# A two-block transformer layer on one core: the pieces beside the attention stream and VectorE's order laid out anew

## The reference

```python
# attention, 16 heads of 8
q = q / jnp.maximum(jnp.linalg.norm(q, axis=-1, keepdims=True), EPS_NORM)   # k too
attn = jnp.einsum('bhqd,bhkd->bhqk', q, k) * scale
attn = jax.nn.softmax(attn, axis=-1)
out = jnp.einsum('bhqk,bhkd->bhqd', attn, v)
...
# feed-forward, 352 wide, every operand in blockwise FP4 (blocks of 16 along the last dim)
gate = fp4_linear(x, w_gate)
y = fp4_linear(x, w_up)
h = jax.nn.silu(gate) * y
return fp4_linear(h, w_down)
...
x = x + _L0_attn_ref(xn, ...) + _L0_ffn_ref(xn, ...)
```

## Time and profile before

| | |
|---|---|
| median of 3 runs | 912.56 us (910.73 to 913.38) |
| the profiled execution | 920.16 us, span 918.0 us, mean granted TensorE clock 0.964 |
| attention stream, first to last exponential | 53.6 to 332.2 us |
| busy in that stretch | ScalarE 240.3, TensorE 237.9, VectorE 148.7 us |
| experts | about 430 to 918 us |

### The profile page before, as it was taken

The page is one execution under the profiler, slowest core; times in us unless marked ns, Lnnn a source line. Parts: engine busy times, 40 slices in busy tenths (PEclk is TensorE's granted clock), DMA queues, the critical chain, the costliest instruction groups (busy, mean ns, idle before and its releaser), DMA issues.

```text
span 918.0 us, 15733 instructions
## 1 busy us (share of the span) xinstructions
PE 826.0 (90%) x4516; PEld 519.7 (57%) x4516; DVE 691.6 (75%) x1413; ACT 701.8 (76%) x1165; POOL 35.2 (4%) x41
## 2 busy tenths in 40 slices
PE   4678998998887789897999999999999999999997
PEld 2421222222221139674777777777777777777775
DVE  5885464334556536974999999999999989999997
ACT  3689898998878645554778888787878778878786
POOL 1700000000000000400000000000000000000000
PEclk9969999999999879998999999999999999999999
DMA  4000000000000000007777777787877778778773
GB/s 117 1 1 1 1 2 1 1 1 1 1 1 0 1 1 2 12 30 185 195 190 196 199 194 197 188 198 193 194 199 193 198 183 204 192 198 199 186 203 96
DMA packets 66776, 99.88 MB, mean 109 GB/s; under 512 B 29270, under 2 KB 45942, under 8 KB 66742
## 3 DMA queue, kind: packets, MB, share of 16 engines
q1 hardware_dynamic: 66742, 99.44, 43.0%
HBM read 97.04 MB, written 2.36 MB: 108 GB/s over the span
## 4 chain that ended last, share of the span: by engine, by line
PE 52%; DVE 17%; DMA 12%; ACT 6%; issue 6%; SPq 5%; DVEq 2%; ACTq 0%
DMA wg_raw<-in_L_ffn_w_gate_dram 11%; PE PS L1134 9%; PE PS L1440 5%; PE PS L1442 5%; PE PS L1441 5%; PE PS L1447 5%; PE PS L1449 5%; PE PS L1448 5%; SPq L224 4%; ACT E L446 4%; PE PS L1120 3%; PE PS L1183 3%; DVE HM L1023 2%; ACT SI L581 2%; PE PS L1419 2%
## 5 line engine op out<-in xcount | busy, mean ns | idle before, releaser
L446 ACT ACTIVATE E<-PS 128x1536 f32<-128x1536 f32 x171 | 235.0, 1472 | 35.3 <-PE PS L1120 35.0
L581 ACT ACTIVATE SI<-PS 128x512 f32<-128x512 f32 x320 | 191.5, 599 | 86.6 <-PE PS L1442 86.5
L1023 DVE TENSOR_TENSOR HM<-SI,CWB 128x512 f32<-128x512 f32 x320 | 221.4, 692 | 40.6 <-ACT SI L581 18.1
L1028 DVE TENSOR_TENSOR HLo<-HM,HH 128x512 fp32r<-128x512 f32 x320 | 218.8, 684 | 0.2
L387 ACT ACTIVATE HH<-HM 128x512 fp32r<-128x512 f32 x320 | 199.4, 623 | 3.9 <-DVE HM L1023 3.9
L1134 PE MATMUL PS<-E,VS 128*32 128x512 f32 x1024 | 145.7, 652 | 14.6 <-DVE OS L761 12.7
L1440 PE MATMUL PS<-XH,wgH 128*128 128x512 f32 x320 | 134.4, 420 | 0.0
L1447 PE MATMUL PS<-HH,wdH 128*128 128x512 f32 x320 | 128.2, 400 | 1.2 <-DVE HLo L1028 1.2
L1441 PE MATMUL PS<-XL,wgH 128*128 128x512 f32 x320 | 126.9, 396 | 0.0
L1449 PE MATMUL PS<-HH,wdL 128*128 128x512 f32 x320 | 126.8, 396 | 0.0
L1442 PE MATMUL PS<-XH,wgL 128*128 128x512 f32 x320 | 126.7, 396 | 0.0
(11 more groups left out here) (221 smaller groups left out, 864.9 us busy)
## 6 DMA issues: line engine op xcount, KB each, us to landing
CWB<-combine_weights SPq DMA_DIRECT2D x320, 256.0 KB, 3.9
wg_raw<-in_L_ffn_w_gate_dram SPq DMA_DIRECT2D x80, 64.0 KB, 3.5
wd_raw<-in_L_ffn_w_down_dram SPq DMA_DIRECT2D x80, 64.0 KB, 3.8
X<-in_L_attn_x_dram SPq DMA_DIRECT2D x4, 256.0 KB, 3.6
combine_weights<-CWT SPq DMA_DIRECT2D x2, 512.0 KB, 2.9
out_dram<-X SPq DMA_DIRECT2D x4, 256.0 KB, 2.9
combine_weights<-CWT SPq DMA_DIRECT2D x2, 128.0 KB, 3.8
qkvw_raw<-in_L_attn_qkv_w_dram SPq DMA_DIRECT2D x1, 192.0 KB, 4.2
```

The lines of the kernel that those rows point to most:

```text
L446: nc.scalar.activation(E[:, g % RING, 0:w, :], PS[:, 3 * (g % 2):3 * (g % 2) + w, :], ACT.Exp, scale=SCALE0).then_inc(S["exp_act"], 1)
L581: nc.scalar.activation(SI[:, slot % 2, :], bank(4 + slot % 2), ACT.Silu).then_inc(S["s_act"], 1)
L1023: TT(HM[:, slot % 4, :], SI[:, slot % 2, :], CWB[:, q, half, CH * c:CH * c + CH], ALU.mult)\
L1028: TT(HLo[:, slot % 4, :], HM[:, slot % 4, :], HH[:, slot % 4, :].bitcast(F32), ALU.subtract)\
```

## The change

Three things. First, the places of the pieces: `SHADE_AT` now holds all 62 of them but the last, at most one in a trio, the outputs' too (`OUT_AT` goes); they run from trio 18 to 170. Second, VectorE's calls are in a new order, which follows that of the pieces. Third, `quantise_hidden` is called for one tile at a time, sixteen times, each set between other calls, and `quantise_gate_up` takes the gate's or the up's weights, one at a time. No arithmetic differs, no data move differs, and the second block is not touched. The new `SHADE_AT` keeps the rule that the keys of a head group are replaced only behind the first batch's last scores with them.

```diff
--- before.py
+++ after.py
@@ -256,21 +256,16 @@
 
 
 
-        SHADE_AT = {25: ("k", 0), 28: ("q", 0), 35: ("w", 0), 36: ("w", 1), 39: ("w", 2), 45: ("k", 1), 46: ("q", 1),
-                    49: ("x", 0), 50: ("x", 1), 56: ("g", 0), 57: ("g", 1), 60: ("u", 0), 62: ("u", 1),
-                    66: ("k", 2), 67: ("q", 2), 68: ("g", 2), 70: ("g", 3), 72: ("u", 2), 74: ("u", 3),
-                    77: ("g", 4), 78: ("g", 5), 81: ("u", 4), 82: ("u", 5), 83: ("x", 2), 84: ("x", 3),
-                    88: ("k", 3), 89: ("q", 3), 90: ("g", 6), 92: ("g", 7), 94: ("u", 6), 95: ("u", 7),
-                    98: ("g", 8), 99: ("g", 9), 103: ("u", 8), 104: ("u", 9),
-                    109: ("g", 10), 110: ("g", 11), 113: ("u", 10), 115: ("u", 11),
-                    119: ("g", 12), 121: ("g", 13), 124: ("u", 12), 126: ("u", 13),
-                    130: ("g", 14), 131: ("g", 15), 135: ("u", 14), 136: ("u", 15)}
-        OUT_AT = {after(NB * m + NB + 2): m for m in range(B * GRP - 1)}
-        SHADE = []
-        for g in range(TRIOS):
-            SHADE += [("o", OUT_AT[g])] if g in OUT_AT else []
-            SHADE += [SHADE_AT[g]] if g in SHADE_AT else []
-        SHADE.append(("o", B * GRP - 1))
+        SHADE_AT = {18: ("x", 0), 22: ("w", 2), 24: ("k", 0), 28: ("w", 0), 30: ("o", 0), 34: ("x", 1), 35: ("g", 0),
+                    39: ("q", 0), 42: ("o", 1), 43: ("k", 1), 44: ("w", 1), 46: ("o", 2), 48: ("g", 1), 50: ("u", 0),
+                    54: ("u", 1), 56: ("g", 2), 59: ("u", 2), 62: ("o", 3), 64: ("q", 1), 66: ("g", 3), 67: ("k", 2),
+                    70: ("g", 4), 71: ("o", 4), 72: ("o", 5), 73: ("u", 3), 75: ("u", 4), 77: ("g", 5), 78: ("o", 6),
+                    79: ("x", 2), 80: ("u", 5), 81: ("g", 6), 84: ("q", 2), 86: ("g", 7), 88: ("u", 6), 89: ("g", 8),
+                    91: ("u", 7), 92: ("q", 3), 95: ("g", 9), 97: ("o", 7), 99: ("u", 8), 102: ("g", 10), 103: ("x", 3),
+                    104: ("k", 3), 106: ("o", 8), 107: ("u", 9), 109: ("g", 11), 112: ("u", 10), 114: ("o", 9), 118: ("u", 11),
+                    120: ("g", 12), 122: ("u", 12), 126: ("o", 10), 130: ("g", 13), 141: ("g", 14), 142: ("u", 13), 146: ("o", 11),
+                    150: ("u", 14), 152: ("g", 15), 158: ("o", 12), 162: ("o", 13), 166: ("u", 15), 170: ("o", 14)}
+        SHADE = [SHADE_AT[g] for g in sorted(SHADE_AT)] + [("o", B * GRP - 1)]
         TANH_AT = {g + 1: w[1] for g, w in SHADE_AT.items() if w[0] == "g"}
 
 
@@ -793,9 +788,9 @@
                 quantise(dn, dn, P, I0 // BLK).then_inc(S["fw_dve"], 1)
                 dve.drain()
 
-            def quantise_gate_up():
-                gu = gu_raw[:, :, :].rearrange("p a (b k) -> p (a b) k", k=BLK)
-                quantise(gu, gu, FP, 2 * FA * D // BLK).then_inc(S["fw_dve"], 1)
+            def quantise_gate_up(w):
+                gu = gu_raw[:, FA * w:FA * w + FA, :].rearrange("p a (b k) -> p (a b) k", k=BLK)
+                quantise(gu, gu, FP, FA * D // BLK).then_inc(S["fw_dve"], 1)
                 dve.drain()
 
             def quantise_x(g):
@@ -833,76 +828,109 @@
                     head_T(t)
             square_sums(3)
 
-            def two_tiles(t, m):
-                output(m - 1)
-                gate_out(t)
-                gate_out(t + 1)
-                divide(m - 1)
-                hidden(t)
-                hidden(t + 1)
-
             second_heads(2)
             second_heads(3)
             quantise_down()
             output(0)
-            quantise_gate_up()
-            divide(0)
+            quantise_x(0)
+            inputs_T(0)
+            quantise_gate_up(0)
+            down_weights()
             output(1)
             second_keys(0)
+            quantise_x(1)
+            gate_up_weights(0)
+            quantise_gate_up(1)
+            divide(0)
+            output(2)
+            inputs_T(1)
+            gate_out(0)
+            quantise_x(2)
+            second_queries(0)
             divide(1)
-            second_queries(0)
-            quantise_x(0)
-            output(2)
-            gate_up_weights(0)
+            second_keys(1)
+            output(3)
             gate_up_weights(1)
             divide(2)
-            down_weights()
-            quantise_x(1)
-            output(3)
-            second_keys(1)
+            gate_out(1)
+            hidden(0)
+            quantise_x(3)
+            hidden(1)
+            output(4)
+            gate_out(2)
+            hidden(2)
+            divide(3)
             second_queries(1)
-            divide(3)
-            inputs_T(0)
-            inputs_T(1)
-            quantise_x(2)
-            two_tiles(0, 5)
-            quantise_x(3)
             output(5)
+            gate_out(3)
             second_keys(2)
+            gate_out(4)
+            divide(4)
+            divide(5)
+            hidden(3)
+            hidden(4)
+            output(6)
+            gate_out(5)
+            divide(6)
+            inputs_T(2)
+            hidden(5)
+            gate_out(6)
+            quantise_hidden(0, 1)
             second_queries(2)
-            gate_out(2)
-            divide(5)
-            gate_out(3)
-            hidden(2)
-            hidden(3)
-            two_tiles(4, 7)
-            inputs_T(2)
+            gate_out(7)
+            output(7)
+            hidden(6)
+            gate_out(8)
+            hidden(7)
+            second_queries(3)
+            quantise_hidden(1, 1)
+            gate_out(9)
+            divide(7)
+            output(8)
+            hidden(8)
+            quantise_hidden(2, 1)
+            gate_out(10)
             inputs_T(3)
-            output(7)
             second_keys(3)
-            second_queries(3)
-            gate_out(6)
-            divide(7)
-            gate_out(7)
-            hidden(6)
-            hidden(7)
-            two_tiles(8, 9)
-            quantise_hidden(0, 2)
-            two_tiles(10, 10)
-            quantise_hidden(2, 2)
-            two_tiles(12, 11)
-            quantise_hidden(4, 2)
-            two_tiles(14, 12)
-            quantise_hidden(6, 2)
+            divide(8)
+            hidden(9)
+            output(9)
+            gate_out(11)
+            quantise_hidden(3, 1)
+            hidden(10)
+            divide(9)
+            quantise_hidden(4, 1)
+            hidden(11)
+            output(10)
+            gate_out(12)
+            hidden(12)
+            quantise_hidden(5, 1)
+            divide(10)
+            quantise_hidden(6, 1)
+            output(11)
+            gate_out(13)
+            quantise_hidden(7, 1)
+            quantise_hidden(8, 1)
+            quantise_hidden(9, 1)
             output(12)
+            gate_out(14)
+            quantise_hidden(10, 1)
+            hidden(13)
+            divide(11)
+            quantise_hidden(11, 1)
+            hidden(14)
+            output(13)
+            gate_out(15)
+            residual()
+            quantise_hidden(12, 1)
             divide(12)
-            quantise_hidden(8, 4)
-            output(13)
+            quantise_hidden(13, 1)
+            output(14)
             divide(13)
-            quantise_hidden(12, 4)
-            output(14)
+            quantise_hidden(14, 1)
+            hidden(15)
+            quantise_hidden(15, 1)
             divide(14)
-            residual()
             output(15)
             divide(15)
 
@@ -1160,7 +1188,7 @@
 
             def gate_up_T(w):
                 o = bank_free("w", w)
-                pe.wait_ge(S["fw_dve"], 2)
+                pe.wait_ge(S["fw_dve"], 2 + w * 1)
                 for a in range(FA):
                     last = TR(o[:, FP * a:FP * a + FP], gu_raw[:, FA * w + a, :], ident[0:FP, 0:FP])
                 last.then_inc(S["shade_pe"], 1)
@@ -1184,10 +1212,10 @@
                    start=True, stop=True).then_inc(S["shade_pe"], 1)
 
             def beside(g):
-                if g in OUT_AT:
-                    out_T(OUT_AT[g])
                 kind, n = SHADE_AT.get(g, (None, None))
-                if kind in ("k", "q"):
+                if kind == "o":
+                    out_T(n)
+                elif kind in ("k", "q"):
                     second_heads_T(kind, n)
                 elif kind == "w" and n < 2:
                     gate_up_T(n)
```

## The result

The changed kernel takes 885.67 us (median of 4 runs, 884.38 to 886.92), the kernel before 912.97 (4 runs, 910.73 to 924.28): a ratio of 0.968, 95% interval 0.960 to 0.976. (A ratio compares the executions of both kernels, without the two on record that were marked slow, and not the two medians, whose quotient is 0.970.) A second set of six executions, with a median of 883.88 us beside 17 of the kernel before with 917.57, gave 0.965 (0.961 to 0.970). The forecast was 887, range 879 to 900.

The account below looks back on a forecast made before the run. ScalarE's exponentials were taken to set the attention stream's pace. Its idle falls from 38.0 to 14.1 us (debt, start, VectorE, clock), saving 23.9, plus 1.6 from overlap: 25.5 off the 912.56 median gives 887 us, range 879 to 900.

Parts of the forecast that it names:

- signs named for being right: Attention stream: stage some 253 us, ScalarE's score waits near 14, copy waits under 3, VectorE busy about 174, one-tile block 4.7.
- signs of being wrong: TensorE waiting at bank 7 or for copies at trios 142, 153, 164; half tanh waits; clock under 0.9 behind 240 us.
- debt at TensorE: Attention stream: TensorE work beyond the trio's pace, above 0.85 us of slack, stops ScalarE 7.2 us after, 13.8 before.
- VectorE's lateness: Attention stream after the change: late VectorE work idles ScalarE 0.7 (trio 36), 0.4 (trio 57) and 1.1 us (trios 142, 164).
- clock: Attention stream: falls to the low clock, two on double steps, one or two elsewhere; 4 us charged, bounds 0 and 9.
- TensorE's ledger: Debt added over 171 trios: above 0.85 us, 11.9 us in 26 trios before, 6.2 in 13 after; this part gives 6.6.
- factor of 1.16: Scaling of the ledger's debt, since trios 57 to 112 gave 5.95 us where the trace has 6.9.
- rival of a clock that falls in the quiet tail: Sparse tail of the attention stream: clock falls cost 5 us more than charged, 892 us; chance 0.13.
- The end stays: End of the attention stage: last exponential, two steps, output, transposes and division stay as before.
- VectorE as the bound of the tail: Behind trio 131: VectorE 55 us against ScalarE's 53.6; three late outputs give back 10.5, 897.5 us; chance 0.15.
- no change: Stage behind attention can't use an earlier end: 912 us; chance 0.03.
- the slower case: Bank 7's single order makes outputs 4 to 14 all late at 3.5 us each: 927 us; chance 0.05.

Follow-up runs that it names:

- experiment 9: Changed kernel again: 883.88 us, 0.965; with the residual moved to trio 62: 885.42, 0.968; with tile 0 also quantised at trio 70: 883.17, 0.964.
- experiment 1: Kernel before, with the quantising of the 16 hidden tiles left out: 896.87 us, 0.977 of the kernel before.
- experiment 4: Kernel before, old places of pieces, hidden tiles quantised one by one from trio 104 on, two in a row behind most groups of pieces: 922.64 us, 1.005.
- experiment 10: Kernel before, with the transposes of output 14 moved from trio 165 to the last trio, 170: 918.96 us, 1.004.
- experiment 3: Changed kernel, with hidden tiles quantised in the groups of before (twos and fours), each where its last tile's call stood: 905.07 us, 0.986 of the kernel before.
- experiment 8: Changed kernel, with hidden tiles quantised two at a time at the place of each second call: 893.17 us, 0.977 of the kernel before.
- experiment 9's third kernel: Changed kernel, with the residual moved to trio 62 and tile 0 quantised at trio 70, each later call taking the next tile: 883.17 us, 0.964.

## Why the prediction was right

**The bound.** Right. ScalarE sets the pace; of 42.9 us that could be had in the profiled execution 31.8 came. Of the signs named for being right the copy waits (2.6 us) and the block of 4.7 us came as told; the stage (246.9 us for 253), ScalarE's waits (8.8 for 14) and VectorE's busy time (164.7 for 174) came lower. Two of the signs of being wrong came too, late copies at trios 142 and 164 and a granted clock under 0.9 behind 240 us (0.65), both small.

**The sum, term by term** (ScalarE's waits after, us):

| term | forecast | measured |
|---|---|---|
| debt at TensorE | 7.2 | 4.1 (9 gaps of 0.19 to 0.78) |
| start at the low clock | 0.65 | 0.9 |
| VectorE's lateness | 2.2 | 2.4 (0.34 at trio 36, none at 57, 1.34 at 142, 0.71 at 164) |
| clock | 4 | 1.4 (2.79 at 142 less the 1.34 of experiment 9) |
| all | 14.1 | 8.8 |

The saving in the stream was thus 31.8 us, not 25.5, with 2.9 more behind it, and that 887 lies so near to 885.67 is luck: a saving forecast too small was taken off a median of three executions (912.56) that was too low for this kernel. In the second set 33.7 us were saved between the medians, as between the two profiles (33.5). The terms that were mis-sized are the debt and the clock, both too high.

**TensorE's ledger.** The mechanism is right, trio by trio: gaps came at trios 36 (the input transposes of the walk, 0.34 for the 0.7 foreseen), 44, 48, 72, 73, 80, 81, 89, 104 and 107 and none was over 0.78. Four of the thirteen foreseen did not show: 79, 92, 97 and 112. Two sizes were off. The ledger counts a gap against the pace of 1.34 us, but ScalarE's idle time starts only when an exponential has run its full 1.45, so each stop shows 0.1 less than its debt: 0.78 foreseen at trios 80 and 81, 0.66 measured, and the two starts of the result's rows are 2.10 us apart (170.22 and 172.32), just the 0.32 + 1.00 + 0.79 of the ledger. (A debt of less than 0.1 cannot show at all; by the ledger's own costs those at 97 and 112 are 0.06 and 0.08.) The sum set this debt beside measured idle time and booked the overlap apart, and so had those 0.1 twice. And the factor of 1.16, taken from trios 57 to 112 of the kernel before, comes mostly from VectorE's lateness there (one gap of 1.52 us at 157.9, behind a key copy that TensorE waited 2.2 us for); it should not have been carried over: without it the ledger's 6.2 us are already more than the 5.1 that came (4.1, and 0.1 for each of the nine gaps). (3.1 x 1.16 is 3.6, not 3.7; nothing hangs on it.)

**The blocks of VectorE.** The forecast that long blocks cost 21 us before is borne out: 22.8 (experiment 1). That their worth is independent of the places is wrong. The prediction costed two parts side by side; the runs show that neither gives its share alone. Places alone 0.986, short blocks alone 0.990 at best and 1.005 at worst, both 0.968 and 0.965: 2.3% by the sum of the single ones, 3.2 to 3.5% together. The intervals are about half a per cent wide to either side, so the surplus is shown less firmly than that short blocks alone do little; and the layouts, three in the old places and one in the new, are mine, another might do better. Without hidden blocks the two sets of places are 14.6 us apart, with the blocks of before some 13 (0.986), with short ones 21 to 23 at the best old layout (906.75 against 885.67 and 883.88).

**VectorE's busy time.** 174 us were forecast, 164.7 came: the 4.72 us of a block are its length with the drains between its instructions, of which 3.95 are busy (67.59 to 72.31 us, the block in rows 8); of the two-tile block's 7.28 it is 6.51, of the four-tile block's 11.79 it is 11.02. The length was right for lateness and wrong for busy time.

**Late copies.** Trio 142: 1.0 us late foreseen, 1.68 us of TensorE's waiting measured; the price to ScalarE was 2.79 and not 0.6. With the same wait and no fall of the clock it is 1.34 (experiment 9), so of the 2.19 us too many 0.74 are a mis-sized lateness and 1.45 the clock, which the sum had charged apart. Trio 164: 0.5 foreseen (what is left of the 1.1) and 0.71.

**The clock.** The price of a fall was right: at the double step of trio 36, with the same instructions, ScalarE stopped 2.14 us where the clock was low and 0.50 in the execution of experiment 4, where it was not, 1.64 us apart. The reason given for the fall, that TensorE had stood idle, does not tell the two apart: in the four microseconds ahead of that trio's scores TensorE was busy 2.55 us in the execution where the clock fell (from 104.46) and 2.56 in the one where it did not (from 103.58), with the same waits of 0.95 and 0.50 us for ScalarE. The number of falls was wrong for this kernel: its tail has one, behind a wait for VectorE, and so has the second execution of it. The rival of a clock that falls in the quiet tail by itself is real but rare: it came once, in the kernel with the residual moved (experiment 9).

**The end.** "The end stays" was wrong by 2.9 us: in the ten microseconds behind the stream the granted clock was 0.55 before (332.2 to 342.2 us) and 1.00 after (300 to 316 us). What causes it is open; experiment 10 tried one cause and did not decide. Its premise, low in the old places and not in the new, does not hold whole: with longer blocks in the new places the clock was low there too (0.50 from 324 to 328 us in experiment 3, 0.69 from 316 to 320 in experiment 8), and with no hidden blocks in the old places as well (0.50 from 312 to 320, experiment 1).

**The rivals.** VectorE as the bound of the tail, the clock in the tail, no change and the slower case did not come. The first is near, though: with blocks of two, 0.977, and of four, 0.986.

## What to carry to other kernels

An engine that works through a fixed list serves two kinds of work, what others wait for and what nobody does; the second kind should be cut into blocks no longer than the slack of the first, even where each cut costs (4.72 us a tile against 2.95), but only if the first kind is spread too; that this is because a block's lateness then meets nothing due at once is the likely reason, not a tested one. Count the slack before cutting: leave the background work out in one run, and the gaps that its engine then shows are the places and the sizes (in the old places, where none in the dense part was as long as a block, blocks so laid gained 1%). A parcel of work beside a paced stream costs nothing in the beats where the pacing engine has room and its full length elsewhere; a ledger of debt, beat by beat, told the larger of such stops to 0.12 us.

## What the runs showed of the hardware that was not expected

- The same instructions, with the same work of TensorE ahead of them (2.55 and 2.56 of 4 us), met the low clock in one execution and not in another. At the double step of trio 36 the kernel before stopped ScalarE for 2.14 us in the profile shown, 0.50 in that of experiment 4; the changed one 0.34, and 1.86 in experiment 9's third kernel, where the granted clock of 104 to 108 us was 0.57. Each such meeting costs about 1.6 us, as much as a late copy. The kernel before spread from 908.6 to 924.3 us in its runs; of the 55 executions beside the experiments the 15 quickest (to 913.4 us) had a mean granted clock of 0.973 to 0.976, and 37 of the other 40 had 0.968 or less.
- VectorE's lateness carried over one to one: 22.8 us added to its blocks in place gave 21.8 us more of TensorE's waiting for copies, 26.1 more of ScalarE's waiting and 28.7 us more in time.
